# A selective-scan stage in which layer-norm sums are kept as interleaved pairs of token chunks, one normalization is folded into the last sum, and scan states are carried two at a time

## The chip, the cores and the metric

The kernel runs on 1 core of a Trainium2 chip. The metric is the device time of one execution in microseconds (us), as the median of several runs. A core has five engines that run at the same time, each through a list of its own in fixed order: TensorE (PE, matrix products, with its weight loads as PEld), VectorE (DVE), ScalarE (ACT), GpSimd (POOL) and SyncE (SP, which here only starts transfers). An instruction waits on semaphores that other engines raise.

## What is computed

4096 tokens of width 256 go through two layers. The change touches only the last stage: the second layer's selective scan, its output projection, a layer norm, then a feed-forward network with its own input norm, and a last layer norm. Cut to that stage, the reference is:

```
xz = x @ w_in.T + b_in; x_ssm, z = split(xz); z = silu(z)
dt = softplus(x_ssm @ w_dt.T + b_dt); Bm, Cm = x_ssm @ w_B.T + b_B, x_ssm @ w_C.T + b_C
h[t] = exp(A * dt[t]) * h[t-1] + dt[t] * Bm[t] * x_ssm[t]        # for each of 16 states n
y[t] = sum over n of h[t] * Cm[t];  y = (y + D * x_ssm) * z
x = layernorm(y @ w_out.T + b_out + x) * gamma + beta            # "norm3"
x = x + (the same x)   ->  x = layernorm(...)                    # "norm4" (the block's input is added)
h = layernorm(x) * ln_gamma + ln_beta                            # "norm5"
x = layernorm(x + (x + 0.5 * (silu(h @ W1 + b1) @ W2 + b2)))     # "norm6"
```

## The kernel before

The stage works in `NB` = 8 blocks of `TB` = 512 tokens. A block has `NC` = 4 chunks of 128 tokens. Two layouts occur: channels on partitions (two halves k of 128 channels, so a tile of 128 x 2 x 512) for the scan, and tokens on partitions (128 x 4 chunks x 256) for the norms.

For each of the `NS` = 16 states n of block b these steps run:

- GpSimd, `into(b, n)` (L2489): state = u * Bm[n], one instruction of 128x1024. It may not start before the product that last read this state buffer is done and that buffer's last column has been saved. There are 3 buffers, so it waits for product n-3.
- ScalarE, `decay(b, n, k)` (L1870): exp(A * dt) for each half k, into one PSUM bank per half, so it waits for the scan of state n-1 on the same half. `spread_C(b, n)` (L1875) copies the row Cm[n] to the one bank `bank_c`, after product n-1.
- VectorE, `scan(b, n, k)` (L2219) for each half, 128x512; then `product(b, n)` (L2225), 128x1024, into one of two buffers `prod`.
- ScalarE, `carry(b, n)` (L1879): saves the last column of the state for the next block in `h0`.
- TensorE, `add_up(b, n)` (L1654): adds the turned product to `bank_y`; product n+2 waits for it.

Around this each block needs: the projections for the next block (`x_proj`, `d_proj`, `bc_proj`, `z_proj` on TensorE, `evac_*` on ScalarE); softplus, shared by ScalarE (`soft_exp`, `plus_one`, `soft_log`, `minus_one`) and GpSimd (`soft_add`, `soft_fix`, `soft_sum`, and `drive`, which makes u); silu of z and the gate (`silu_z` L1926, `gate` L2231); `d_term` (L1645), `turn_gated` (L1662), `evac_gated` (L1931) and `out_proj`; and the norms. For a norm, VectorE takes `bn_stats` of each chunk and `bn_aggr` of each result, GpSimd makes scale and shift (`norm3`, `norm6` of four tiny steps, `norm45` of ten), ScalarE applies them, and GpSimd applies gamma, beta and the added input (`shifted` L2494, `scaled` L2553, `summed` L2559). Last comes `up_proj`, `silu_up` (L1964), `down_proj` and `second` (L2263).

The order on each engine is written out by hand, in a loop over iterations in which blocks at different ages (`cur`, `post`, `last`, `old`) are interleaved. Exp, Silu and Ln need different tables on ScalarE; each change of table is an instruction ACT_TABLE_LOAD, put in where the order of functions asks for it. After the loop, the last block is finished in halves by the `end_*` functions.

## Time and profile before

| | us |
|---|---|
| median of 3 runs | 1187.65 (1184.77 to 1187.85) |
| the profiled execution | 1185.47 |
| its span | 1183.4 |
| PE busy in the span | 1045.4 (88%) |
| DVE busy | 959.9 (81%) |
| ACT busy | 893.4 (75%) |
| POOL busy | 738.1 (62%) |

The span runs from the first to the last instruction; 2.1 us of the execution lie outside it. Busy shares are averages over stages. The changed stage takes the time from 572.7 us to the end.

### The profile page before, as it was taken

The page shows a single profiled execution, that of the slowest core. Times are in us where ns is not written, and L with a number is a line of the kernel's source. Part 1 is how long each engine was busy: PE and PEld are TensorE (multiplying, and loading weights), DVE is VectorE, ACT ScalarE, POOL GpSimd, SP SyncE. Part 2 cuts the span into 40 slices and gives each one's busy share as a digit, 9 for nine tenths or more (in the row PEclk, how much of TensorE's full clock was granted, in tenths as well). Part 3 has the DMA queues.
Part 4 walks back from the last instruction along what each step waited for, and adds up shares of the span by engine and source line. Part 5 has one row for each costly group of instructions (what it writes and reads, how often), then busy time and mean ns, then how long its engine had stood idle before and what let it go on. Part 6 is the DMA issues. An engine that isn't in the chain of part 4 may idle for free. (4 is left out here: it accounts for less than half of the span.)

```text
span 1183.4 us, 17445 instructions
## 1 busy us (share of the span) xinstructions
PE 1045.4 (88%) x5234; PEld 698.0 (59%) x5234; DVE 959.9 (81%) x1319; ACT 893.4 (75%) x1697; POOL 738.1 (62%) x638
## 2 busy tenths in 40 slices
PE   5999999999968999998476599999999999988987
PEld 4677677676753334444245357667575766756576
DVE  5999999999962576545689989999999999999741
ACT  7878787887644455556777889999898999986743
POOL 1546554654560443534568997979889897988420
PEclk9999999999998999999678899999999999999899
DMA  4543434323405001112866546556565565645201
GB/s 128 153 135 109 122 104 130 112 82 114 126 29 180 1 18 54 37 36 91 211 137 172 123 136 150 143 135 149 151 143 139 151 158 135 148 133 142 67 5 36
DMA packets 93232, 133.83 MB, mean 113 GB/s; under 512 B 8786, under 2 KB 47698, under 8 KB 93140
## 3 DMA queue, kind: packets, MB, share of 16 engines
q1 hardware_dynamic: 93140, 132.73, 41.6%
q8 instruction: 42, 0.69, 0.2%
q14 instruction: 50, 0.41, 0.1%
HBM read 116.45 MB, written 14.16 MB: 110 GB/s over the span
## 5 line engine op out<-in xcount | busy, mean ns | idle before, releaser
L2219 DVE TENSOR_TENSOR_SCAN state<-bank_a,h,state 128x512 f32<-128x512 f32 x256 | 316.4, 1270 | 27.5 <-POOL state L2489 12.4
L2489 POOL TENSOR_TENSOR state<-uc,Bb 128x1024 f32<-128x1024 f32 x64 | 150.7, 2367 | 35.3 <-DVE prod L2225 25.9
L2489 POOL TENSOR_TENSOR state<-s,Bb 128x1024 f32<-128x1024 f32 x64 | 150.7, 2367 | 28.2 <-DVE prod L2225 19.7
L1654 PE MATMUL bank_y<-ident,prod 128*128 128x128 f32 x1024 | 138.5, 282 | 28.5 <-DVE prod L2225 28.4
L1654 PEld LDWEIGHTS bank_y<-ident,prod 128*128 128x128 f32 x1024 | 122.8, 145 | 68.3 <-DVE prod L2225 35.8
L2225 DVE TENSOR_TENSOR prod<-state,bank_c 128x1024 f32<-128x1024 f32 x128 | 154.2, 1204 | 6.4 <-ACT bank_c L1875 4.2
L1699 PE MATMUL bank_m<-w,f_h 128*128 128x256 f32 x448 | 106.1, 387 | 0.0
L39 PE MATMUL bank_m<-nT,w 128*128 128x512 f32 x224 | 103.8, 602 | 0.9 <-ACT nT L1953 0.9
L1870 ACT ACTIVATE bank_a<-s,A 128x512 f32<-128x512 f32 x128 | 86.2, 680 | 12.6 <-DVE state L2219 12.5
L1870 ACT ACTIVATE bank_a<-dtc,A 128x512 f32<-128x512 f32 x128 | 86.4, 681 | 10.4 <-DVE state L2219 10.2
L1699 PEld LDWEIGHTS bank_m<-w,f_h 128*128 128x128 f32 x448 | 83.5, 192 | 15.8 <-issue 5.8
L1875 ACT ACTIVATE bank_c<-Cb 128x512 f32<-128x512 f32 x128 | 75.2, 588 | 15.1 <-DVE prod L2225 15.0
L668 DVE TENSOR_TENSOR_SCAN L<-abc,zeros,b_id 128x512 f32<-128x512 f32 x64 | 78.4, 1267 | 5.8 <-POOL xd L871 3.6
L1309 DVE TENSOR_SCALAR cS<-cS,slope,shift 128x512 f32<-128x512 f32 x24 | 13.1, 545 | 67.5 <-ACT cS L1221 67.5
L39 PEld LDWEIGHTS bank_m<-nT,w 128*128 128x128 f32 x224 | 40.8, 193 | 39.0 <-issue 37.4
L333 PE MATMUL b_op<-W_out,zs 128*128 128x256 f32 x256 | 63.1, 389 | 0.0
L896 POOL TENSOR_TENSOR rms<-ssn,mhalf 128x1 f32<-128x1 f32 x32 | 17.8, 555 | 63.8 <-DVE ssn L697 63.8
L635 DVE SCALAR_TENSOR_TENSOR b_p<-raw,columns,b_p 128x512 f32<-128x512 f32 x72 | 54.1, 752 | 1.3
L871 POOL TENSOR_TENSOR xd<-xs,L 128x512 f32<-128x512 f32 x32 | 33.9, 1059 | 31.6 <-PE b_new L321 15.1
L39 PE MATMUL c<-h,nets 128*128 128x512 f32 x96 | 46.7, 609 | 3.7 <-ACT h L1202 3.6
L39 PE MATMUL b_p<-uh,W_h 128*128 128x512 f32 x132 | 46.8, 436 | 2.8 <-DVE ul L721 2.1
L333 PEld LDWEIGHTS b_op<-W_out,zs 128*128 128x128 f32 x256 | 46.2, 190 | 4.9
(388 smaller groups left out, 2595.9 us busy)
## 6 DMA issues: line engine op xcount, KB each, us to landing
Bb<-CB_rows SPq DMA_DIRECT2D x128, 256.0 KB, 4.1
Cb<-CB_rows SPq DMA_DIRECT2D x128, 256.0 KB, 4.7
abc<-decays SPq DMA_DIRECT2D x32, 512.0 KB, 4.7
Ebc<-ramps SPq DMA_DIRECT2D x64, 128.0 KB, 3.2
uT<-in_uT SPq DMA_DIRECT2D x8, 512.0 KB, 4.3
u<-in_u SPq DMA_DIRECT2D x8, 512.0 KB, 4.3
x_tokens<-x2s SPq DMA_DIRECT2D x8, 512.0 KB, 2.9
x_rows<-x1T SPq DMA_DIRECT2D x8, 512.0 KB, 2.7
```

The costliest lines, as they stand in the source:

```text
L39: i = e.matmul(out, w, x, start=(n == 0), stop=(n == len(pairs) - 1))
L333: i = e.matmul(b_op[:, 0:DM], zs[b % 2][:, m, ts], W_out[:, m, :], start=(m == 0), stop=(m == MD - 1))
L635: e.scalar_tensor_tensor(to, raw[:, m, t:t + TB], cw[:, m, t:t + 1], acc[:, :], ALU.mult, ALU.add).then_inc(v_conv, 1)
L668: e.tensor_tensor_scan(L[:, hs, :].rearrange("p h t -> p (h t)"), abc[g % 2][:, hs, :].rearrange("p h t -> p (h t)"), b_id[:, :], zeros[:, ...
L871: e.tensor_tensor(heads(xd[:, :]), heads(xs[g % 2][:, :]), L[:, :, CH - 1:CH].to_broadcast([P, NH, HD]), ALU.mult).then_inc(p_xd, 1)
L1654: i = e.matmul(p_y[c // 2][:, at:at + P], prod[n % 2][:, k, c * CH:(c + 1) * CH], ident[:, :], start=False, stop=(n == NS - 1), is_transpo ...
L1699: i = e.matmul(to, f_h[:, k, c * CH:(c + 1) * CH], w2[:, k, :], start=False, stop=(c % 2 == 1 and k == KF - 1))
L1870: e.activation(p_a[k][:, :], dtc[b % 2][:, k, :], ACT.Exp, scale=A[:, k, n:n + 1]).then_inc(a_a, 1)
L1875: e.activation(p_c[:, :], Cb[n % 4][:, :], ACT.Copy).then_inc(a_c, 1)
L2219: e.tensor_tensor_scan(s[:, k, :], p_a[k][:, :], s[:, k, :], h0[:, n, k:k + 1], ALU.mult, ALU.add).then_inc(v_s, 1)
L2225: e.tensor_tensor(prod[n % 2][:, :, :], state[(NS * b + n) % 3][:, :, :], both(p_c[:, :]), ALU.mult).then_inc(v_g, 1)
L2489: e.tensor_tensor(state[at % 3][:, :, :], uc[b % 2][:, :, :], both(Bb[n % 4][:, :]), ALU.mult).then_inc(p_b, 1)
```

## The change

It edits the scan stage only and does five things.

1. The tiles `xl` and `x3b` hold two token chunks interleaved word by word (2 pairs x 256 features x 2 chunks). One `bn_stats` over the 512 words of a pair then yields the statistics of both chunks, since that instruction reports even and odd elements apart. Six `bn_stats` of 512 take the place of twelve of 256 per block, and the twelve `bn_aggr` go. Whoever writes or reads one chunk of these tiles does it with a step of two words (8 bytes): `residual`, `second`, norm3, norm5, norm6, `scaled`, `summed`.
2. `norm4` is no longer applied by ScalarE. `second` multiplies `xl` by the per-token scale `rs4d` (twice rs4) while it adds; the constant shift drops out of the last norm. It becomes four instructions of 128x256 with a scale read from a column, instead of two of 128x512 with the constant 2.0. One tiny step (`rs4d`) is added to GpSimd's `norm45`. `xl` gets a second buffer.
3. There are 4 state buffers instead of 3 (`into` waits for product n-4), and `carry` saves two states with one instruction, after the odd one's scan; `into` waits for the pair. A wait on a carry covers both of its states.
4. The last norm writes a tile of its own, `x4`.
5. The order is a new one on all five engines.

The diff, cut:

```diff
-            state, prod = many("state", [P, KD, TB], 3), many("prod", [P, KD, TB])
+            states, prod = t("states", [P, 4, KD, TB]), many("prod", [P, KD, TB])
+            state = [states[:, i, :, :] for i in range(4)]
+            rs4d = many("rs4d", [P, NC])
...
+            xl_twos, x3b_twos = [t(n, [P, 2, DM, 2])[:, :, :, :] for n in ("xl0", "xl1")], t("x3b", [P, 2, DM, 2])[:, :, :, :]
+            xl, x3b = [x.rearrange("p q f c -> p q c f") for x in xl_twos], x3b_twos.rearrange("p q f c -> p q c f")
...
                 def carry(b, n):
-                    e.wait_ge(v_s, 2 * (NS * b + n) + 2)
-                    e.activation(h0[:, n, :], state[(NS * b + n) % 3][:, :, TB - 1], ACT.Copy).then_inc(a_hs, 1)
+                    at = NS * b + n
+                    e.wait_ge(v_s, 2 * at + 4)
+                    e.activation(h0[:, n:n + 2, :], states[:, at % 4:at % 4 + 2, :, TB - 1], ACT.Copy).then_inc(a_hs, 1)
...
-                def norm4(b, p):
-                    e.wait_ge(p_l4, 9 * b + 9)
-                    after(e, v_x3b, 2 * b)
-                    for c in (2 * p, 2 * p + 1):
-                        e.activation(x3[:, c, :], xl[:, c, :], ACT.Identity, bias=nb4[:, c:c + 1], scale=rs4[:, c:c + 1]).then_inc(a_x3, 1)
...
-                def stats4(b, c):
+                def stats4(b, p):
                     e.wait_ge(p_add, b + 1)
-                    e.bn_stats(st4[:, c, :], xl[:, c, :]).then_inc(v_l4, 1)
-
-                def mean4(b, c):
-                    e.wait_ge(v_l4, 8 * b + c + 1)
-                    e.sem_inc(step, 1)
-                    e.bn_aggr(mv4[:, c, :], st4[:, c, :]).then_inc(v_l4, 1)
+                    after(e, p_l4, 9 * b)
+                    e.bn_stats(st4[:, p, :], both_of(xl_twos[b % 2], p)).then_inc(v_l4, 1)
 
                 def second(b, p):
                     e.wait_ge(pe_dn, 2 * b + p + 1)
-                    e.wait_ge(a_x3, 4 * b + 4)
-                    after(e, st_o, DMAS * b)
-                    e.scalar_tensor_tensor(x3b[:, 2 * p:2 * p + 2, :].rearrange("p c f -> p (c f)"), x3[:, 2 * p:2 * p + 2, :].rearrange("p c f -> p (c f)"),
-                                           2.0, pair[p][:, :], ALU.mult, ALU.add).then_inc(v_x3b, 1)
+                    after(e, a_n6, 4 * b)
+                    for c in (0, 1):
+                        at = 2 * p + c
+                        i = e.scalar_tensor_tensor(one(x3b, at), one(xl[b % 2], at), rs4d[b % 2][:, at:at + 1], pair[p][:, c * DM:(c + 1) * DM], ALU.mult, ALU.add)
+                    i.then_inc(v_x3b, 1)
...
                 def into(b, n):
...
-                    after(e, v_g, at - 2)
-                    after(e, a_hs, at - 2)
+                    after(e, v_g, at - 3)
+                    after(e, a_hs, (at - 4) // 2 + 1)
...
                     e.tensor_tensor(rs5[:, :], rs4[:, :], sq4[:, :], ALU.mult)
+                    e.tensor_scalar(rs4d[b % 2][:, :], rs4[:, :], 2.0, None, ALU.mult)
...
                 def scaled(b):
                     e.wait_ge(a_n3, 4 * b + 4)
                     e.sem_inc(step, 1)
-                    e.tensor_tensor(xl, xl, rowwise(gam), ALU.mult).then_inc(p_gam, 1)
+                    e.tensor_tensor(xl[b % 2], xl[b % 2], every(gam), ALU.mult).then_inc(p_gam, 1)
```

Below, the order at three places of a block, once before and once in the change. Names are those of tiles without buffer numbers; `x2`, `x3` read as `x`, `st3` as `st`, `s12` as `s`.

GpSimd, first part of a block, before: five `into`, then `shifted` (x<-x), norm6, an `into`, norm3.

```order
L2489 TENSOR_TENSOR state<-s,Bb 128x1024 x5
L2494 TENSOR_TENSOR x<-x,everywhere 128x1024
L2513 TENSOR_SCALAR ve<-mv 128x4
L2516 TENSOR_TENSOR rs<-ve,mhalf 128x4
L2519 TENSOR_TENSOR nb<-mv,rs 128x4
L2522 TENSOR_SCALAR nb<-nb 128x4
L2489 TENSOR_TENSOR state<-s,Bb 128x1024
L2499 TENSOR_SCALAR ve<-mv 128x4
```

In the change:

```order
L2432 TENSOR_TENSOR states<-s,Bb 128x1024 x6
L2437 TENSOR_TENSOR x<-x,everywhere 128x1024
L2442 TENSOR_SCALAR ve<-st 128x4
L2445 TENSOR_TENSOR rs<-ve,mhalf 128x4
L2448 TENSOR_TENSOR nb<-st,rs 128x4
L2451 TENSOR_SCALAR nb<-nb 128x4
L2432 TENSOR_TENSOR states<-s,Bb 128x1024 x2
```

A sixth `into` moved ahead of `shifted`, and norm6 (L2513 to L2522) moved away from here.

GpSimd, from the end of norm45 to the first `into` of the next block, before: `into` 11, `soft_add`, `into` 12 and 13, `soft_fix`, 14, `soft_sum`, 15, `drive`, and on.

```order
L2548 TENSOR_TENSOR nb<-nb,sq 128x4
L2489 TENSOR_TENSOR state<-s,Bb 128x1024
L2564 TENSOR_TENSOR s<-s 128x1024
L2489 TENSOR_TENSOR state<-s,Bb 128x1024 x2
L2570 TENSOR_TENSOR s<-s,uc 128x1024
L2489 TENSOR_TENSOR state<-s,Bb 128x1024
L2576 TENSOR_TENSOR dtc<-dtc,s 128x1024
L2489 TENSOR_TENSOR state<-s,Bb 128x1024
L2582 TENSOR_TENSOR uc<-dtc,xc 128x1024
L2489 TENSOR_TENSOR state<-uc,Bb 128x1024 x5
```

In the change, after the two `into` that now follow norm45:

```order
L2508 TENSOR_TENSOR s<-s 128x1024
L2432 TENSOR_TENSOR states<-s,Bb 128x1024
L2456 TENSOR_SCALAR ve<-st 128x4
L2459 TENSOR_TENSOR rs<-ve,mhalf 128x4
L2462 TENSOR_TENSOR nb<-st,rs 128x4
L2465 TENSOR_SCALAR nb<-nb 128x4
L2432 TENSOR_TENSOR states<-s,Bb 128x1024 x2
L2514 TENSOR_TENSOR s<-s,uc 128x1024
L2432 TENSOR_TENSOR states<-s,Bb 128x1024
L2520 TENSOR_TENSOR dtc<-dtc,s 128x1024
L2526 TENSOR_TENSOR uc<-dtc,xc 128x1024
L2432 TENSOR_TENSOR states<-uc,Bb 128x1024 x6
```

Between norm45 and the next block's first `into` there is one `into` more (number 10), and norm6 (L2456 to L2465) now stands here.

ScalarE, the silu functions of a block, before (`silu_up` three times, `silu_z`, `spread_C`, `silu_up`, then the table of Exp again):

```order
L1964 ACT_TABLE_LOAD
L1964 ACTIVATE f_h<-f_h 128x1024 x3
L1926 ACTIVATE zgs<-zgs 128x1024
L1875 ACTIVATE bank_c<-Cb 128x512
L1964 ACTIVATE f_h<-f_h 128x1024
L1870 ACT_TABLE_LOAD
```

In the change:

```order
L1948 ACT_TABLE_LOAD
L1948 ACTIVATE zgs<-zgs 128x1024
L1980 ACTIVATE f_h<-f_h 128x1024
L1896 ACTIVATE bank_c<-Cb 128x512
L1891 ACT_TABLE_LOAD
```

and 13 rows further on:

```order
L1980 ACT_TABLE_LOAD
L1980 ACTIVATE f_h<-f_h 128x1024 x3
L1896 ACTIVATE bank_c<-Cb 128x512
L1891 ACT_TABLE_LOAD
L1891 ACTIVATE bank_a<-dtc,A 128x512
```

One stretch became two, with two table loads more per block; the 13 rows between them are the next scans' work (six `decay`, two evacuations each of gT and xc, `spread_C`, two `carry`).

## Rows read from the trace of the kernel before

**Rows 1.** Busy time by engine, one steady block; the first line names the columns.

```profile
core 0: us, PE busy (x) PEld busy (x) DVE busy (x) ACT busy (x) POOL busy (x), PEclk, DMA share, GB/s
915.50:984.40 68.90, 65.27 (x317) 45.67 (x316) 65.54 (x79) 64.34 (x115) 60.72 (x41) 1.00 0.61 149
```

**Rows 2.** Instructions on bank_y, the gates: ns min/median/max, first and last start.

```profile
L2231 DVE TENSOR_TENSOR zgs<-bank_y,zgs x16: 662/679/691, 640.1 to 1121.0; 128x512 f32<-128x512 f32 x16
```

**Rows 3.** Chain that ended last: start us, us, what.

```profile
874.47 2.39 POOL xl L2559
```

**Rows 4.** Timeline of POOL: start us, us, instruction, count [idle before <-releaser].

```profile
852.55 2.37 POOL L2489 TENSOR_TENSOR state<-uc,Bb 128x1024 f32<-128x1024 f32 x1 [2.89 <-DVE prod L2225]
854.88 2.37 POOL L2494 TENSOR_TENSOR x<-x,everywhere 128x1024 f32<-128x1024 f32 x1
...
860.48 2.37 POOL L2489 TENSOR_TENSOR state<-uc,Bb 128x1024 f32<-128x1024 f32 x1 [0.89 <-ACT h L1879]
862.94 0.23 POOL L2499 TENSOR_SCALAR ve<-mv 128x4 f32<-128x4 f32 x1
...
865.18 4.71 POOL L2489 TENSOR_TENSOR state<-uc,Bb 128x1024 f32<-128x1024 f32 x2
...
881.60 0.23 POOL L2527 TENSOR_SCALAR ve<-mv 128x4 f32<-128x4 f32 x1
...
886.68 2.36 POOL L2489 TENSOR_TENSOR state<-uc,Bb 128x1024 f32<-128x1024 f32 x1
...
907.83 7.03 POOL L2489 TENSOR_TENSOR state<-s,Bb 128x1024 f32<-128x1024 f32 x3 [0.20 <-POOL s L2582]
```

**Rows 5.** Timeline of DVE, the first row one block earlier than the others.

```profile
841.19 3.63 DVE L2219 TENSOR_TENSOR_SCAN state<-bank_a,h,state 128x512 f32<-128x512 f32 x3
...
860.22 2.56 DVE L2219 TENSOR_TENSOR_SCAN state<-bank_a,h,state 128x512 f32<-128x512 f32 x2 [0.93 <-ACT h L1879]
...
878.91 1.38 DVE L2252 BATCH_NORM_STATS2 st<-xl 128x6 f32<-128x256 f32 x4
880.21 0.41 DVE L2257 BATCH_NORM_AGGREGATE mv<-st 128x2 f32<-128x6 f32 x4
```

**Rows 6.** Groups by line: count | busy us, mean ns | idle before, releasers.

```profile
L2225 DVE TENSOR_TENSOR prod<-state,bank_c 128x1024 f32<-128x1024 f32 x128 | 154.2, 1204 | 6.4 <-ACT bank_c L1875 4.2 <-PE bank_y L1654 0.6 <-DVE state L2219 0.2
...
L2263 DVE SCALAR_TENSOR_TENSOR x3b<-x,bank_m 128x512 f32<-128x512 f32 x14 | 9.5, 683 | 1.6 <-PE bank_m L1699 1.6
...
L1879 ACT ACTIVATE h<-state 128x2 f32<-128x2 f32 x128 | 24.7, 193 | 1.5 <-DVE state L2219 1.5
```

**Rows 7.** Groups by line, the first layer's residual, whose scale is a column.

```profile
L704 DVE SCALAR_TENSOR_TENSOR r<-b_op,rms,u 128x256 f32<-128x256 f32 x32 | 15.2, 475 | 4.6 <-POOL rms L896 4.6
```

**Rows 8.** Timeline of ACT: evacuations of gT, silu functions and table loads, norm5.

```profile
846.81 1.08 ACT L1931 ACTIVATE gT<-bank_m 128x512 f32<-128x512 f32 x2 [0.22 <-PE bank_m L1662]
...
849.08 0.58 ACT L1875 ACTIVATE bank_c<-Cb 128x512 f32<-128x512 f32 x1
...
851.42 1.28 ACT L1964 ACT_TABLE_LOAD   x1
...
859.39 0.69 ACT L1870 ACTIVATE bank_a<-dtc,A 128x512 f32<-128x512 f32 x1
...
886.76 2.07 ACT L1942 ACTIVATE xn<-xl,nb,rs 128x256 f32<-128x256 f32 x4 [1.25 <-POOL nb L2548]
```

**Rows 9.** Timeline of PE: `turn_gated` and `d_term`.

```profile
846.06 1.09 PE L1662 MATMUL bank_m<-ident,zgs 128*128 128x128 f32 x8
...
852.56 1.95 PE L1645 MATMUL bank_y<-diagD,xc 128*128 128x128 f32 x16
```

**Rows 10.** Groups by line, an earlier stage in which POOL and DVE both read two SBUF tiles.

```profile
L1326 DVE TENSOR_TENSOR ob<-oa,tw 128x512 f32<-128x512 f32 x8 | 13.1, 1638 | 0.3
...
L1416 POOL TENSOR_TENSOR oa<-oa,tw 128x512 f32<-128x512 f32 x8 | 12.4, 1552 | 34.2 <-DVE tw L1314 34.0
```

**Rows 11.** Timeline of PE: three pieces of `down_proj` in a row.

```profile
876.97 5.45 PE L1699 MATMUL bank_m<-w,f_h 128*128 128x256 f32 x24
```

636 lines of the change are left out of this document (288 added, 348 removed).

## The prediction, made before the result was known

> **What bounds the kernel now.** I read the busy time by block first. In a steady block of 68.9 us PE is busy 65.3, DVE 65.5, ACT 64.3 and POOL 60.7 us, at a PE clock of 1.00 [rows 1]. No engine is full and three are above 93%, so the question is which loop closes last. The gates run once per block, the first at 640.1 and the last at 1121.0: seven intervals, 68.7 us each on average [rows 2]. Then the chain of waits: it goes through ACT's silu stretch, DVE, and from `summed` on through POOL without a break to the next block's first scan [rows 3]. POOL's timeline shows the loop. Before `shifted` POOL waits 2.89 us for a product, and then 0.89 us for a carry [rows 4]; from 881.60, where norm45 starts, it never waits for another engine: norm45 takes 5.1 us, then ten instructions of 2.33 us (a state after another starts so far apart: 7.03 for three) end at 907.83 + 2.35 = 910.2, and the next block's first scan starts there. With the scan's start at 841.19 [rows 5] as zero, the loop reads: 40.4 us until norm45 + 5.1 + 23.5 = 69.0 us, the block. So POOL, the least busy engine, sets the period by the second half of its list, and DVE, ACT and PE idle 3 to 5 us each. What counts is when norm45 can start, and what stands behind it.
>
> **The change, part by part** (per block; no transfer is added, and the loads' waits for `into` come earlier).
>
> *Statistics.* Four bn_stats take 1.38 us, (1.38 - 0.41) / 3 = 0.325 apart; four bn_aggr 0.41, about 0.09 apart [rows 5]. Twelve of each: 3.9 + 1.1 = 5.0 us. The 512-wide form is not in the trace. Below it lies the 256-wide one (0.325), above two of them (0.65); I take 0.60, the pitch of the 512-wide 0.683 us addition less an overlap of 0.08 [rows 6]. Six: 3.6 us. Gain 1.4, bounds 1.1 to 3.0.
>
> *`second`.* Two of 0.683 become four with a column as scale; that form took 475 ns [rows 7], 0.40 apart. 4 x 0.40 - 2 x 0.60 = +0.4. DVE gains 1.0 us: 64.5.
>
> *ACT.* norm4 goes: four of the kind of norm5, 2.07 for four [rows 8], -2.0. Eight carries of 0.193 us [rows 6], which cost their 0.10 pitch, go: -0.8. Two table loads come: 1.28 each [rows 8], and since nothing overlaps with one, 1.39; +2.8. ACT stays at 64.3: the loads eat what the norm gave.
>
> *POOL.* One tiny step in norm45, +0.17. PE: nothing but its order.
>
> *Steps of 8 bytes.* No wide instruction of the trace steps over words. Below: nothing (a gain has no cause, the words are as many). Above: the dearest rows of such a kind, where both engines fight for SBUF: a 512-wide DVE instruction 1.64 us instead of 0.68, a 512-wide POOL one 1.55, so 3.10 for 1024 words against 2.37 [rows 10, 4]. I take nothing, since the nearest row, the same instruction without a step, knows no such rival here; the upper end is a rival below.
>
> The Trainium skill speaks against that choice in one place: *Vector Engine (DVE) Microarchitecture Reference*, section "Measured stream behaviour on trn2", states that a port streams at full rate only in runs of two adjacent words, and that a hop at every word costs about 0.65 cycle; its page *SBUF — State Buffer*, section "Door 1: The DMA port swizzle", says that fp32 may be strided up to four words for free. By the first `residual` and `second` would cost DVE some 1.6 us more per block (an estimate from that page) and eat its gain, with ACT and POOL perhaps alike, which is the last rival below; by the second they would cost nothing. No row here decides.
>
> *The loop, anew.* Zero is again the block's first scan. (a) DVE's list to product 5: 16 scans at (3.63 - 1.27) / 2 = 1.18 = 18.9; six products at 1.12 (1.204 less 0.08) = 6.7; gates, residuals and norm3's statistics, two each at 0.60 = 3.6; half of `second` 0.8. Together 30.0. Into it come waits. The gates end at 3.65; then PE runs `d_term` 1.8 (moved ahead of `turn_gated`), and turns 1.1 [rows 9], so at 6.0 ACT evacuates gT, with decays between, then `spread_C` and the first pair's carry: 3.05 us (the like stretch took 849.66 - 846.81 = 2.85, [rows 8]), until 9.05. Two decays and an evacuation more: 10.9. Then ACT's second silu stretch: load, three silus, `spread_C`, load = 6.2 us (the one before took 8.0, 851.42 to 859.39) until 17.1, so the next scan starts at 17.8. DVE's own list gets there at 16.8: 1.0 us of wait, in place of the 0.93 there [rows 5]. Two waits of 0.2 for decays before that. Product 4 waits for `add_up` 2, which PE has behind four pieces of `down_proj`, 7.3 us (three take 5.45, [rows 11]), and a `d_proj`: 0.6. Decay 7 stands behind `soft_exp`: 0.2. The last two are my reading of two lists side by side, good to half a microsecond each. Sum 2.2, so product 5 ends at 32.2. (b) POOL: `into` 4 waits for the pair's carry at 9.05, `into` 5 follows, `shifted` at 13.8 (before: 854.88 - 841.19 = 13.7), norm3 to 18.4 (2.24, [rows 4]), `into` 6 and 7, `scaled`, `summed`, `into` 8 = 5 x 2.33, with 1.25 of waits for product 3 and ACT's norm3: 31.5. So `into` 9 waits for product 5: 32.2. What stood in the way before, norm6 and an `into` between `shifted` and norm3, 865.18 - 857.3 less norm3 = 5.6 us, is gone. (c) From there: `into` 9 2.33, norm45 5.25, then 11 wide instructions 25.6 and norm6 2.25: 67.7. Norm6, free before because it stood where POOL waits, is now paid on the path, and so is `into` 10.
> I add 0.3 for handovers that I didn't count: **68.0 us a block, 1.0 less** than the 69.0 that the same reckoning gives before. Four buffers alone gain nothing there: the path runs over carry and norm45, not over a state buffer.
>
> *Sum.* Seven intervals: -7.0. First block: silu_z's loads come before its second state instead of its third, the softplus part has more products to run behind it: -0.5. End: after the last matmul 2 bn_aggr (0.25 with their handovers) and half a bn_stats overlap go, the two-part `second` costs 0.2 more [rows 5 to 7]: -0.3. Together -7.8. The profiled execution was 1185.47, its span 1183.4; the median stands 2.2 above it. On the median: 1187.65 - 7.8 = 1179.9, rounded **1180**.
>
> **Rivals.**
> *POOL alone (faster).* If DVE's four waits shrink, `into` 9 starts at 31.5 at once and the handovers cost nothing: 67.0 us, 2.0 less, 1187.65 - 14 - 0.8 = 1173. For it: each wait is small, and PE's share (65.3) allows it. If it packs better still, PE's 65.3 is the floor: 1162.
> *No change.* The loop gains nothing if the waits in (a) are 3.2 instead of 2.2, with three engines above 93%: two silu stretches leave DVE without decays twice. Then 68.7 to 69.0: 1186 to 1188.
> *The pair's carry (slower).* `into` 4 waits for a carry which in ACT's list stands behind both gT evacuations, these behind `turn_gated`, that behind `d_term` and the gates. A carry at 9.05 is just right; from 10.1 on the block is as long as before, since all of (b) follows it 1:1 once POOL passes product 5. Were it at 11.5, the block would be 69.4, and a late `into` 4 also starts the scans later: +0.5 x 7 and more, 1192. POOL's wait of 2.89 us at this place [rows 4] shows how much hangs there.
> *The steps cost (slower).* `scaled` and `summed` lie on POOL's path; at 3.10 instead of 2.37 the block grows by 1.5, ACT's four norm3 and DVE's second `residual` add 0.5: 2.0 x 7 = 14, less 7.8: 1194. It decides from 0.5 us per pass, a fifth of its 2.37.
> The Trainium skill's DVE page, section "Measured stream behaviour on trn2", points this way.
>
> **How the numbers follow.** A measurement of this kernel tells about 0.3% (3.6 us) from no change. Forecast (1174 to 1184) 0.40; POOL alone and better 0.18; no change 0.18; pair's carry 0.12; steps 0.12. Faster 0.58, same 0.18, slower 0.24. The range leaves out half of the two outer ends: 1168 to 1195.
>
> **What would show it.** A gate interval near 68.0; norm45 starting some 35 us after a block's first scan instead of 40.4, and the first scan still waiting for its `into` (POOL) at the block's end; norm6 among POOL's unbroken work; 6 table loads per block; DVE near 64.5 busy, ACT unchanged. `scaled` at 2.37 and `residual` at 0.68 prove the steps free. I'm wrong in my main step if the first scan doesn't wait for POOL, or if norm45 starts later than 36 or earlier than 33.

## The result, and the profile after

The changed kernel takes 1193.01 us, the kernel before 1187.22 in the same measurement: a ratio of 1.0048, 95% interval 1.0035 to 1.0060. It is 0.5% slower; I had forecast 0.6% faster (1180). The profiled execution of the changed kernel took 1192.86, its span 1190.9, 7.5 more than the 1183.4 of before. (The profiled execution of one experiment, old_order_s6, ran at a lower clock throughout, so the trace read in its place is that of the same kernel made again, old_order_s6_b.)

Two windows of the changed kernel, each from gates to gates. The columns are those of [rows 1]:

```profile
core 0: us, PE busy (x) PEld busy (x) DVE busy (x) ACT busy (x) POOL busy (x), PEclk, DMA share, GB/s
853.30:922.40 69.10, 65.85 (x314) 45.32 (x314) 64.14 (x64) 64.27 (x105) 61.12 (x42) 1.00 0.53 146
922.40:993.20 70.80, 67.34 (x314) 46.99 (x314) 64.18 (x63) 64.67 (x105) 61.08 (x42) 0.98 0.61 142
```

The same view in windows of 5 us, one row of it:

```profile
925.00:930.00 5.00, 5.00 (x21) 3.76 (x20) 3.27 (x3) 3.13 (x6) 3.95 (x2) 0.69 0.64 126
```

DVE fell from 65.5 us [rows 1] to 64.15, a little more than I said, and ACT stayed. But a clean block takes 69.08, not 68.0, and one block takes 70.8: in it PE's granted clock was 0.69 for five microseconds, between its two levels.

The difference of 7.5 us, by place, from the first scan and the gates in the two timelines, one profiled execution of each kernel:

| Stretch | before | after | difference | forecast |
|---|---|---|---|---|
| start of the stage's first scan | 575.27 | 576.13 | +0.9 | 0 |
| from there to the first gates | 64.8 | 71.3 | +6.5 | -0.5 |
| seven intervals of gates | 480.3 | 481.8 | +1.5 | -7.0 |
| last gates to the end of the span | 63.0 | 61.6 | -1.4 | -0.3 |

The seven intervals hold a first one that is 0.9 longer (67.7 against 66.8), one dip of the clock (+2.1 against before), a last interval that is 2.0 shorter, and otherwise blocks of 69.08 instead of 68.8 to 69.1. The start of the stage moved between 573.0 and 579.4 in the experiments, whatever they changed: that 0.9 is no part of the change. One execution is a coarse measure of the second row too: without a stall this stretch took 62.7 to 65.6 us in the experiments, and 63.2 and 65.6 in two executions of one kernel (old_order and its repeat). The medians below say the same with less noise.

**The first block.** PE, ACT, DVE and POOL of the changed kernel at the start of the stage. Columns: start us, us, instruction, count, [idle before <- what ended it]:

```profile
584.10 3.78 PE L39 MATMUL bank_m<-xT,w_xz 128*128 128x512 f32 x4 [15.30 <-DMA xT<-x_rows]
587.68 3.15 PE L1667 MATMUL bank_y<-diagD,xc 128*128 128x128 f32 x16
```

```profile
580.31 1.30 ACT L1891 ACTIVATE bank_a<-dtc,A 128x512 f32<-128x512 f32 x2
590.86 0.69 ACT L1908 ACTIVATE xc<-bank_m,columns 128x512 f32<-128x512 f32 x1 [9.25 <-PE bank_y L1667]
```

```profile
581.11 2.46 DVE L2219 TENSOR_TENSOR_SCAN states<-bank_a,h,states 128x512 f32<-128x512 f32 x2 [1.26 <-ACT bank_a L1891]
592.23 2.46 DVE L2219 TENSOR_TENSOR_SCAN states<-bank_a,h,states 128x512 f32<-128x512 f32 x2 [8.67 <-ACT bank_a L1891]
```

```profile
593.65 4.69 POOL L2432 TENSOR_TENSOR states<-uc,Bb 128x1024 f32<-128x1024 f32 x2 [10.86 <-ACT h L1901]
```

Four engines stand still. In the new list of PE `x_proj(1, 0)` stands ahead of `d_term(0)`; it needs the second block's `xT`, which lands at 584.1. ACT's evacuation of it (L1908) waits for `d_term(0)` and stands ahead of decay 2, DVE's scan 2 waits for that decay, and POOL for a carry.

**A clean block.** DVE from its first scan to product 5, and POOL from `into` 2 to norm45, in the changed kernel:

```profile
850.91 2.46 DVE L2219 TENSOR_TENSOR_SCAN states<-bank_a,h,states 128x512 f32<-128x512 f32 x2 [1.08 <-POOL states L2432]
...
868.84 2.46 DVE L2219 TENSOR_TENSOR_SCAN states<-bank_a,h,states 128x512 f32<-128x512 f32 x2 [0.83 <-ACT h L1901]
...
877.85 1.22 DVE L2225 TENSOR_TENSOR prod<-states,bank_c 128x1024 f32<-128x1024 f32 x1 [0.62 <-PE bank_y L1676]
...
882.81 1.22 DVE L2225 TENSOR_TENSOR prod<-states,bank_c 128x1024 f32<-128x1024 f32 x1 [0.19 <-PE bank_y L1676]
```

```profile
855.11 4.70 POOL L2432 TENSOR_TENSOR states<-uc,Bb 128x1024 f32<-128x1024 f32 x2 [1.97 <-ACT h L1901]
860.45 4.69 POOL L2432 TENSOR_TENSOR states<-uc,Bb 128x1024 f32<-128x1024 f32 x2 [0.65 <-ACT h L1901]
...
884.20 2.38 POOL L2432 TENSOR_TENSOR states<-uc,Bb 128x1024 f32<-128x1024 f32 x1 [1.13 <-issue]
886.66 0.19 POOL L2470 TENSOR_SCALAR ve<-st 128x4 f32<-128x4 f32 x1
```

The shape is the forecast one. With the first scan at 850.91 as zero, `into` 4 starts at 9.5 (forecast 9.05), `into` 9 waits for product 5 (the row with 1.13; the trace names no releaser, but the product ended at 884.03, 0.17 earlier), norm45 starts at 35.75 (34.55; 40.4 before), and from there POOL runs on to the next first scan, which waits for it (1.08). But product 5 ends at 33.1, not 32.2, and behind norm45 (4.8; forecast 5.25) POOL needs 28.4, not 27.9.

PE in the same block of the changed kernel:

```profile
854.60 2.05 PE L1667 MATMUL bank_y<-diagD,xc 128*128 128x128 f32 x16 [1.90 <-DVE zgs L2231]
856.49 1.04 PE L1684 MATMUL bank_m<-ident,zgs 128*128 128x128 f32 x8
...
867.95 7.17 PE L1721 MATMUL bank_m<-w,f_h 128*128 128x256 f32 x32
874.96 1.88 PE L39 MATMUL bank_m<-xc,w_dt 128*128 128x512 f32 x4
876.68 1.04 PE L1676 MATMUL bank_y<-ident,prod 128*128 128x128 f32 x8
```

From `d_term` on none of its rows has a wait. The last row is `add_up` 2, for which product 4 waits: 23.1 us of PE work stand between the gates and product 4. The next `add_up` ends 5.0 us of PE work later, and product 5 waits for it in turn (0.19).

### The profile page after: what moved, and what is told of

Read it like the earlier page. It is cut to its first block and busy times, and to the rows that moved or that the text cites. A ratio compares the mean times of both kernels' runs of the same rounds, so it can differ in the third digit from the quotient of the medians.

```text
span 1190.9 us, 17184 instructions
## 1 busy us (share of the span) xinstructions
PE 1053.6 (88%) x5234; PEld 705.4 (59%) x5234; DVE 948.9 (80%) x1193; ACT 888.6 (75%) x1613; POOL 739.8 (62%) x645
## 5 line engine op out<-in xcount | busy, mean ns | idle before, releaser
L2219 DVE TENSOR_TENSOR_SCAN states<-bank_a,h,states 128x512 f32<-128x512 f32 x256 | 315.2, 1268 | 35.1 <-ACT bank_a L1891 24.2
L2432 POOL TENSOR_TENSOR states<-uc,Bb 128x1024 f32<-128x1024 f32 x64 | 150.5, 2367 | 36.1 <-ACT h L1901 19.3
L2225 DVE TENSOR_TENSOR prod<-states,bank_c 128x1024 f32<-128x1024 f32 x128 | 154.2, 1205 | 19.0 <-PE bank_y L1676 11.3
L2432 POOL TENSOR_TENSOR states<-s,Bb 128x1024 f32<-128x1024 f32 x64 | 150.5, 2366 | 22.6 <-ACT h L1901 13.4
L1676 PEld LDWEIGHTS bank_y<-ident,prod 128*128 128x128 f32 x1024 | 122.2, 146 | 58.3 <-DVE prod L2225 27.9
L1721 PE MATMUL bank_m<-w,f_h 128*128 128x256 f32 x448 | 102.4, 382 | 0.0
L39 PEld LDWEIGHTS bank_m<-nT,w 128*128 128x128 f32 x224 | 39.7, 190 | 39.7 <-issue 34.9
```

What stands on the lines that cost most here:

```text
L39: i = e.matmul(out, w, x, start=(n == 0), stop=(n == len(pairs) - 1))
L1676: i = e.matmul(p_y[c // 2][:, at:at + P], prod[n % 2][:, k, c * CH:(c + 1) * CH], ident[:, :], start=False, stop=(n == NS - 1), is_transpo ...
L1721: i = e.matmul(to, f_h[:, k, c * CH:(c + 1) * CH], w2[:, k, :], start=False, stop=(c % 2 == 1 and k == KF - 1))
L2219: e.tensor_tensor_scan(s[:, k, :], p_a[k][:, :], s[:, k, :], h0[:, n, k:k + 1], ALU.mult, ALU.add).then_inc(v_s, 1)
L2225: e.tensor_tensor(prod[n % 2][:, :, :], state[(NS * b + n) % 4][:, :, :], both(p_c[:, :]), ALU.mult).then_inc(v_g, 1)
L2432: e.tensor_tensor(state[at % 4][:, :, :], uc[b % 2][:, :, :], both(Bb[n % 4][:, :]), ALU.mult).then_inc(p_b, 1)
```

## Experiments

Each kernel was timed beside the kernel before (here with its own ratio), and "block us" is the usual interval of gates among the middle five of its profiled execution, those with a dip of the clock left out.

| Kernel | median us | ratio, 95% | block us |
|---|---|---|---|
| changed kernel | 1193.0 | 1.0048 (1.0035 to 1.0060) | 69.08 |
| fix_first | 1185.1 | 0.9978 (0.9962 to 0.9995) | 69.06 |
| before_stall | 1193.9 | 1.0053 (1.0033 to 1.0073) | 68.8, 69.1 |
| fix_x_twice | 1186.5 | 1.0000 (0.9984 to 1.0016) | 69.08 |
| fix_norm6 | 1183.8 | 0.9960 (0.9946 to 0.9975) | 68.8 |
| fix_silu | 1196.6 | 1.0071 (1.0045 to 1.0098) | 69.8; three with a dip, 71.1 to 71.4 |
| fix_norm6_silu | 1190.3 | 1.0023 (1.0006 to 1.0039) | 69.65 |
| fix_silu22 | 1188.6 | 1.0018 (1.0002 to 1.0034) | 69.08, 69.4, 69.85; two with a dip |
| fix_norm6_silu22 | 1186.2 | 1.0004 (0.9990 to 1.0019) | 69.7 |
| fix_single | 1188.4 | 1.0008 (0.9992 to 1.0023) | 69.06 |
| before_four | 1180.9 | 0.9949 (0.9933 to 0.9964) | 68.04 |
| before_four_pairs | 1180.1 | 0.9941 (0.9926 to 0.9956) | 67.98 |
| before_four_into5 | 1182.7 | 0.9953 (0.9936 to 0.9970) | 68.01 |
| old_order | 1179.8 | 0.9949 (0.9929 to 0.9969) | 67.84 |
| old_order_b, the same again | 1182.0 | 0.9956 (0.9939 to 0.9973) | 67.83 |
| old_order_into5 | 1182.5 | 0.9966 (0.9954 to 0.9978) | 67.84 |
| old_order_s6 | 1183.5 | 0.9963 (0.9948 to 0.9978) | not read |
| old_order_s6_b, the same again | 1182.4 | 0.9962 (0.9948 to 0.9977) | 67.74 |
| old_order_three | 1186.0 | 0.9983 (0.9969 to 0.9997) | 68.33 |

**1. The first block.** One kernel takes the early projection back in the first block alone, the other puts it, in the first block alone, into the kernel before.

```diff
# fix_first: PE of the changed kernel (x_proj(1, 1) and d_proj(1, ...) likewise, and ACT's evacuations to match)
-                    if 0 < cur < NB:
+                    if 1 < cur < NB:
                         x_proj(cur, 0)
                     if live(post):
                         d_term(post)
...
                     if live(post):
                         add_up(post, 0)
+                    if cur == 1:
+                        x_proj(cur, 0)
```

```diff
# before_stall: PE, then ACT, of the kernel before
+                    if cur == 1:
+                        x_proj(cur, 0)
                     if live(post):
                         d_term(post)
...
+                    if nxt == 1:
+                        evac_x(nxt, 0)
                     if live(cur):
                         carry(cur, 0)
                         decay(cur, 2, 0)
```

> The changed kernel, but in the first block alone PE does x_proj(1,0) after add_up(0,0) and x_proj(1,1) after add_up(0,1) (and d_proj(1,0), (1,1) after add_up 2 and 3), and ACT evacuates them behind carry(0,2), decay(0,5,0), decay(0,6,0) and carry(0,4), roughly as the kernel before did. Theory A (a load at the head of the line: x_proj(1,0) waits for the xT load until 584.1 and holds d_term(0), add_up(0,0), ACT's decay 2, DVE and POOL): the first gate comes at 640 to 641.5 instead of 647.4, the median falls by 6 to 7.5 us to 1186 +- 1, the same as the kernel before. Rival B (the first block is long because of silu_z's early table loads and the carries in pairs, which stay): the first gate stays at 645 to 648 and the time at 1191 to 1193.

> The kernel before, with one move in the first block alone: x_proj(1,0) ahead of d_term(0), and its evacuation ahead of ACT's carry(0,0) and decay(0,2,0). Theory A: the first gate moves from 640.1 to 646 to 648 and the time rises by 6 to 8 us, to about 1194. Rival B (the load's wait is hidden, and something else in the new order costs): 1187 to 1189, first gate at 640 to 642.

fix_first is 0.7% below the changed kernel's ratio, and from its first scan (575.78) to its first gates (641.0) it takes 65.3 us instead of 71.3; 64.8 was before's. before_stall rises from 1187.2 to 1193.9; from its first scan (579.40) to the first gates (652.8) it takes 73.4, in an execution (1198.2) that was 4 us above its median. Its trace has the same rows: PE, then ACT.

```profile
587.88 3.44 PE L39 MATMUL bank_m<-xT,w_xz 128*128 128x512 f32 x4 [15.17 <-DMA xT<-x_rows]
```

```profile
593.14 0.69 ACT L1888 ACTIVATE xc<-bank_m,columns 128x512 f32<-128x512 f32 x1 [10.56 <-PE bank_y L1645]
```

One instruction placed ahead of its data, once in the run, costs 6.6 us in the one kernel and about 8 in the other, by the medians: more than the whole difference between the two. silu_z's early table loads (rival B) cost nothing that stands clear of the spread of this stretch.

**2. The dips of the clock.** fix_x_twice computes `x_proj(b, 0)` twice from block 2 on, where PE waits 1.90 us for the gates:

```diff
+                    if m == 0 and b > 1:
+                        passes(e, single[:, :], [(w_xz[...], xT[:, k, :]) for k in range(KD)])
                     passes(e, single[:, :], [(w_xz[...], xT[:, k, :]) for k in range(KD)]).then_inc(pe_x, 1)
```

> fix_first, with x_proj(b, 0) of the blocks 2 to 7 computed twice in a row (the second overwrites the first; four 128x512 matmuls, 1.88 us at 2.4 GHz, behind add_up 15), where PE waits 1.90 us for the gates. Theory C (a clean block costs 69.07 whatever PE does there, and the two dips to 1.2 GHz behind that wait, 1.5 and 1.75 us in two blocks, come because PE stands still): no interval above 69.3 among the third to the sixth, which saves about 3.3 us in a profiled run; the median 1 to 3 us below fix_first's 1185.1. Rival Q (PE's work is the bound): each block grows by up to 1.9, and the time rises by 5 to 12 us. Rival D (the dips come whatever PE does): intervals of 70.6 stay, time within 1 us of fix_first.

fix_first's profiled execution had two blocks of 70.6 and 70.8; in fix_x_twice the same blocks are 69.09 and 69.39 (a little above the 69.3 of theory C), with a clock of 1.00, and the wait is 0.19 instead of 1.90:

```profile
918.29 2.05 PE L1669 MATMUL bank_y<-diagD,xc 128*128 128x128 f32 x16 [0.19 <-DVE zgs L2249]
```

So 1.9 us more of PE work there is free (rival Q falls). The other traces speak for theory C as well. Five kernels have a PE wait of 1.9 to 2.2 us at the gates from their third block on (the changed kernel, fix_first, fix_silu, fix_silu22, fix_single); 9 of their 20 blocks of this kind show a dip, each right behind the gates. The other profiled kernels wait about 1.0 us or less there (fix_x_twice, the three with norm6 moved, all that have the order of before), and none of their middle blocks shows one. But the median of fix_x_twice is 0.2% above fix_first's, not below. What the dips cost on average stays open. What one dip does is plain, and it matters below. DVE in the changed kernel's block with the clock at 0.69:

```profile
948.43 1.22 DVE L2225 TENSOR_TENSOR prod<-states,bank_c 128x1024 f32<-128x1024 f32 x1 [0.62 <-PE bank_y L1676]
```

Product 4 comes 28.43 us after this block's first scan (920.00) instead of 26.94, still with 0.62 us of wait for PE: what PE loses to the clock between the gates and `add_up` 2 (1.5 us), the block loses (1.8 in all).

**3. What closes the loop in the new order.** All with the first block mended. fix_norm6 moves POOL's norm6 out of the tail behind norm45 to where POOL waits 1.97 us; fix_silu merges ACT's two stretches of silus (two table loads fewer per block); fix_norm6_silu does both; silu22 moves one silu from the second stretch to the first; fix_single saves each state by itself, the first of a pair earlier.

```diff
# fix_norm6, POOL (ACT's second norm6 goes behind spread_C 3)
                         into(cur, 1)
+                    if 0 <= old < NB - 2:
+                        norm6(old)
...
                         into(cur, 12)
-                    if 0 <= last < NB - 2:
-                        norm6(last)
# fix_norm6, ACT
                         decay(cur, 1, 1)
+                    if 0 <= old < NB - 2:
+                        norm6(old, 0)
...
                         evac_x(nxt, 0)
```

```diff
# fix_silu, ACT
-                        silu_z(cur)
-                        silu_up(last, 0)
...
+                        silu_up(last, 0)
                         silu_up(last, 1)
                         silu_up(last, 2)
                         silu_up(last, 3)
+                        silu_z(cur)
```

> fix_first, and POOL's norm6 of block b moved from behind into 12 of block b+2 to behind into 1 of block b+3, where POOL waits 1.97 us for a carry; ACT's norm6 ahead of evac_x (1.27 us of wait there) and behind spread_C 3. Theory P (POOL still closes the loop: the block's first scan waits 1.08 us for it): the 2.25 us of norm6 leave POOL's saturated half, the interval between gates falls from 68.9 by about 1.1 to 67.8, where DVE or PE takes over, so about 7 us below fix_first: 1179. Rival Q (PE, 65.9 us busy with a 1.9 us wait for the gates in each block and clock dips after it, already sets the period): the interval stays at 68.6 to 69.0 and the time at 1185 to 1187.

> fix_first, with silu_z and silu_up 0 moved from the block's start into the second stretch of silus: one stretch of load, five silus, load instead of two, so two table loads fewer per block (2.6 us of ACT). If the long stretch starves DVE (it lasts 1.28 + 3.9 + 1.06 + 1.28 = 7.5 us and more instead of 6.2, but nothing stands ahead of the first scan): scan 4 comes about 1.3 to 2 us later and the interval grows by 0.5 to 1.2 us: time 1190 to 1194. If ACT's total is what binds: interval 67.5 to 68, time 1178 to 1180. If neither, within 2 us of fix_first.

> fix_norm6 with the silus in one stretch, as fix_silu had them (interval 71.1). Theory T (in the new order ACT's stretch, product 5, into 9, norm45 and the 13 steps behind it are one loop, so its terms add): norm6 gone from the tail takes 2.0 to 2.25 off 71.1, interval 68.9 to 69.2, time 1184 to 1187. Rival U (the stretch closes a loop of its own through scan, gates and gT, in which norm6 has no part): 70.5 to 71.2, time 1194 to 1197.

> fix_first, with silu_up 1 in ACT's first stretch of silus instead of the second: stretches of 3 and 2 silus instead of 2 and 3, table loads as many. In the changed kernel scan 4 waits 0.83 us behind the second stretch, while ACT waits 1.27 us for PE behind the first. If the loop runs through ACT's second stretch to product 5, into 9 and norm45: interval 69.07 - 0.5 to 0.8 = 68.3 to 68.6, 3 to 5 us below fix_first: 1180 to 1182. If the carry into 2 (then 0.95 later) or another wait takes over: within 1.5 us of fix_first.

> fix_norm6 with the same move of silu_up 1. There POOL no longer closes the loop (its carry wait at into 13 is 1.21 us), and DVE waits 0.34, 0.94, 0.82 and 0.45 us for ACT in the first 22 us of a block. If it is ACT's second stretch that holds DVE: scan 4's 0.82 goes, interval 68.75 - 0.8 = 68.0, time 1178 to 1179. If ACT's whole list up to soft_exp is what holds DVE (no ACT wait stands in it but 0.32): the wait only moves between the stretches, 68.6 to 68.9, time 1183 to 1185.

> fix_first with a carry for each state instead of each pair (8 more per block on ACT, 0.8 us), carry 14 ahead of silu_z and carry 0 ahead of the evacuations of gT, so that into 2 (1.97 us of wait) and into 4 (0.65) can run earlier. If the pair's late release is what binds (theory K): interval 68.0 to 68.5, time 1179 to 1182. If product 5 and what comes behind it bind (into 9 waits 1.13 us for it in a clean block): POOL's waits move to shifted and into 9, interval 69.0 to 69.4, time within 2 us of fix_first.

*norm6 off the tail.* 69.06 becomes 68.8, not 67.8, and the median is 1.3 us below fix_first's, not 7. But this kernel did two things at once. On POOL 2.25 us left the tail, and the first scan no longer waits for POOL; DVE's list has taken over, and from product 5 to the next first scan it takes 34.9 us instead of 36.0. On ACT the first half of norm6 (1.12 us) moved ahead of the evacuation of `x_proj`, and now PE waits for that evacuation in a stretch that had no wait. PE, then DVE, in fix_norm6 (first scan at 842.50):

```profile
849.86 1.98 PE L39 MATMUL bank_m<-xT,w_xz 128*128 128x512 f32 x4 [0.75 <-ACT xc L1916]
```

```profile
870.28 1.22 DVE L2241 TENSOR_TENSOR prod<-states,bank_c 128x1024 f32<-128x1024 f32 x1 [0.58 <-PE bank_y L1676]
```

Product 4 starts 27.8 us after the first scan instead of 26.9. So 1.1 us were won behind product 5 and 0.8 lost ahead of product 4; the 0.3 are the difference, and no run shows norm6 moved on POOL alone. fix_norm6_silu22, which missed both of its expectations, puts one silu more ahead of the same evacuation. PE in it (first scan at 840.96):

```profile
849.26 1.98 PE L39 MATMUL bank_m<-xT,w_xz 128*128 128x512 f32 x4 [1.69 <-ACT xc L1916]
```

Product 4 starts at 28.7, and the block grows from 68.8 to 69.7, by what product 4 came later.

*One stretch of silus.* At full clock the block is 69.8, 0.75 longer than fix_first's. The 71.1 on which the expectation of fix_norm6_silu was built is a block with a dip of the clock; three of this kernel's five middle blocks had one. Two windows of fix_silu, one with a dip and one without, columns as in [rows 1]:

```profile
849.35:920.53 71.18, 67.29 (x314) 46.91 (x314) 63.81 (x63) 62.00 (x102) 61.09 (x42) 0.98 0.54 142
991.59:1061.39 69.80, 64.11 (x310) 44.72 (x310) 63.81 (x64) 61.79 (x102) 61.07 (x42) 1.00 0.54 137
```

With norm6 moved as well a block takes 69.65, without a dip: 0.15 less than 69.8, not 2.0 to 2.25. So neither theory T nor rival U is borne out, and the two table loads saved brought nothing. In both kernels with one stretch DVE waits ahead of product 4 for the later silus (1.80 us ahead of product 2, 0.83 ahead of scan 4), and product 4 no longer waits for PE.

*The other two.* Moving a silu took away scan 4's wait and put 1.55 us ahead of scan 2; single carries took away POOL's wait ahead of `into` 2 and put 2.31 ahead of `into` 4. fix_single's blocks stayed at 69.0 to 69.1 bar one dip, and the shortest of fix_silu22 is 69.08. Their ratios are 0.3 and 0.4% above fix_first's all the same; fix_silu22 had blocks of 69.4 and 69.85 besides, and for fix_single the trace doesn't show why. DVE in fix_silu22 (a block with a dip; in one without, product 4 waits 0.62 too), then in fix_single:

```profile
848.51 2.46 DVE L2235 TENSOR_TENSOR_SCAN states<-bank_a,h,states 128x512 f32<-128x512 f32 x2 [1.55 <-ACT bank_a L1899]
...
868.04 1.22 DVE L2241 TENSOR_TENSOR prod<-states,bank_c 128x1024 f32<-128x1024 f32 x1 [0.62 <-PE bank_y L1676]
```

```profile
870.87 1.22 DVE L2251 TENSOR_TENSOR prod<-states,bank_c 128x1024 f32<-128x1024 f32 x1 [0.62 <-PE bank_y L1676]
```

In every kernel that kept two stretches of silus, product 4 waits for PE: 0.62 in the changed kernel, in its block with the slow clock, with a silu moved and with single carries, 0.58 in fix_norm6. So the loop reads: gates, PE's 23.1 us to `add_up` 2, product 4, product 5, `into` 9, norm45, POOL's 28.4, first scan, gates. What ACT, DVE or the carries gain ahead of product 4 doesn't shorten it as long as PE doesn't wait for them. Made longer, PE's part shows in the block each time: by a dip (product 4 1.5 us later), by ACT's norm6 (0.8) and by norm6 and a silu (1.8). That a shorter list of PE there would give the time back was not run; this half is argued, not shown.

**4. Buffers and carries alone.** The kernel before with four state buffers; the same with the carries in pairs; the same with `into` 5 behind `into` 4:

```diff
-            state, prod = many("state", [P, KD, TB], 3), many("prod", [P, KD, TB])
+            state, prod = many("state", [P, KD, TB], 4), many("prod", [P, KD, TB])
...
-                    after(e, v_g, at - 2)
-                    after(e, a_hs, at - 2)
+                    after(e, v_g, at - 3)
+                    after(e, a_hs, at - 3)
```

> The kernel before with four state buffers instead of three, nothing else. My prediction: nothing gained there, since its loop runs over the carry and norm45; interval 68.6 to 68.9, time 1186.5 to 1188. Rival: POOL's waits for a product before into are on the path (2.89 us before shifted), and a fourth buffer takes one of them away: interval lower by 0.5 to 2 us, time 1175 to 1184.

> The kernel before with four state buffers (an interval of 68.03 us) and the carries in pairs, each pair at the place of its odd carry in ACT's list; nothing else. Theory K (the pair gives back what the fourth buffer brought, since slot and carry are released two states at a time, and the interval of the changed kernel, 69.09, is 1.05 above that of before_four for it): interval 68.8 to 69.3, time 1186 to 1190. Rival L (POOL has 3.24 us of idle time ahead of shifted, which takes a later release; the 8 carries fewer give ACT 0.8 us): interval 67.9 to 68.2, time 1179 to 1182, and the 1.05 lies in the order and the two more table loads of the changed kernel.

> before_four with into 5 moved from behind norm6 to behind into 4, where POOL waits 3.24 us for a residual. POOL's unbroken run, from norm6 to the next block's scans, gets 2.35 us shorter. If POOL closes the loop of before_four (one wait of 0.52 us of DVE for a state is left in it): the interval falls until DVE's own list binds, 65.5 us of work and 1.9 of waits for ACT and PE: 67.4 to 67.6, about 3.5 us less in all, 1176 to 1178. If DVE binds there already: 68.0, within 1 us of before_four.

My statement that four buffers alone gain nothing is wrong: they give 0.8 us a block and 0.5%. POOL in before_four:

```profile
849.73 2.39 POOL L2494 TENSOR_TENSOR x<-x,everywhere 128x1024 f32<-128x1024 f32 x1 [3.24 <-DVE xl L2238]
```

The waits for a product and a carry of [rows 4] (2.89 and 0.89) are gone; what is waited for is the residual, and then the statistics of norm6 (1.31). norm45 starts 0.8 us earlier after the first scan, at 39.6. The carries in pairs, my slower rival, cost nothing: the release comes later (a new wait of 1.36 for a carry), and the 3.24 shrink to 1.81. `into` 5 moved into that gap brings nothing either: 0.47 us of wait for the statistics appear ahead of norm45.

**5. The new instructions in the old order.** old_order is the changed kernel (its buffers, statistics, `second`, carries in pairs) with every engine's list in the order of before up to the end of the loop: an instruction that is gone is left out, and a statistic of a pair stands where those of its chunks stood. Behind the loop its lists are those of the changed kernel. The other three move one to three entries of it:

```diff
# s6, DVE
                         scan(post, 10, 0)
-                    if 0 <= old < NB - 2:
-                        stats6(old, 0)
...
                         stats3(post, 1)
+                    if 0 <= old < NB - 2:
+                        stats6(old, 0)
# into5, POOL; "three" has both, and norm4's statistics ahead of scan(post, 8, 1)
                         into(cur, 4)
+                        into(cur, 5)
                     if 0 <= post < NB - 1:
                         shifted(post)
```

> The changed kernel's buffers and instructions (interleaved pairs, one statistics instruction for each, norm4 in the last sum, carries in pairs, four states), but every engine's list in the order of the kernel before, first block included. Theory O (the new order is what costs, the new instructions bring the 1.0 us of DVE that I predicted): norm45 can start earlier by what DVE saves ahead of it, 0.6 to 1.0, so an interval of 67.1 to 67.5 against 68.0 for before_four_pairs, time 1174 to 1177. Rival Y (the new instructions cost on the path what they save, by steps of 8 bytes or by waits): 68.0 or more, time 1180 or more. Rival P (POOL's unbroken run from norm6 on, which does not depend on DVE's savings, holds it at 68.0): 67.9 to 68.1.

> old_order with into 5 behind into 4, ahead of shifted, where POOL waits for a residual. If POOL's run from norm6 on held old_order, 0.5 to 1.0 us per block less than that, 1170 to 1174. If DVE's list up to the statistics of norm4 holds it, no change (within 1.5 us of old_order), as it was for before_four_into5.

> old_order_s6 again. Theory S (the saved work had been cover): DVE's wait for decay 4 is 1.1 to 1.2 us, the interval 67.2 to 67.4, 3 to 4 us less than old_order on the same chip. Rival (the next wait takes it up: the median of the disturbed run, 1184.5, points this way): interval 67.7 to 68.2, the time within 2 us of old_order.

> old_order_s6 with into 5 ahead of shifted, and the statistics of norm4 one scan (1.2 us) earlier in DVE's list, ahead of scan(8,1). If two loops hold the block, both are eased now: norm45 can start up to 1.2 us earlier, and DVE's list with its waits is 64.4 + 2.7 = 67.1: interval 67.0 to 67.4, a gate sum about 3 to 4 us below old_order's, time 1177 to 1179. If ACT's norm3 ahead of scaled (1.8 us of wait there in old_order_into5) or another wait holds it: 67.6 to 67.9, within 1.5 us of old_order.

old_order takes 67.84, 0.14 less than before_four_pairs, though DVE has 0.9 us less to do (64.4 busy against 65.25). Where it went, in its DVE:

```profile
855.78 2.47 DVE L2212 TENSOR_TENSOR_SCAN states<-bank_a,h,states 128x512 f32<-128x512 f32 x2 [1.81 <-ACT bank_a L1887]
```

The wait for the decay behind ACT's stretch of silus has grown from 0.93 (in before_four and in before_four_pairs) to 1.81. From the gates (840.30) to this scan it is 15.48 us, and in before_four (840.85 to 856.33) the same 15.48: all that the statistics and `second` save ahead of scan 4 is waited away there. Moving another statistic there (s6) cut the wait to 1.38 and the block to 67.74: 0.1, not 0.6, because DVE then waits 0.71 for POOL's last states; its median is that of old_order's repeat. `into` 5 ahead of `shifted` changes nothing (67.84). Both together, with norm4's statistics earlier, gave 68.33 (old_order_three), worse: now ACT waits 1.61 us for PE's turned gates, where it waited 0.95 in old_order.

```profile
844.59 1.09 ACT L1949 ACTIVATE gT<-bank_m 128x512 f32<-128x512 f32 x2 [1.61 <-PE bank_m L1679]
```

old_order's block is shorter than that of before_four_pairs, yet the kernel isn't faster: from the last gates to the end it takes 66.9 us (66.9 to 67.2 in all five executions of this family), where before_four_pairs takes 63.5 and the changed kernel 61.6. The end part and the lists were not written for each other. ACT's list behind the loop is the changed kernel's, with two silus ahead of the last evacuation of the gates; before has them behind it. In the changed kernel the table load and the silus begin before the last gates, in old_order ACT first has norm6 to do at that point, and PE waits for the evacuation, 3.66 us where before_four_pairs has 0.77:

```profile
1116.87 0.79 PE L1622 MATMUL bank_c<-bias,ones 64*128 64x512 f32 x1 [3.66 <-ACT gT L1988]
```

DVE's first instruction behind it starts 10.2 us after the last gates instead of 5.3 (changed kernel 4.7). The 3.4 us that its end is longer than that of before_four_pairs come from there, as far as these rows show; a kernel with before's order there wasn't run. Its block is what speaks about the new instructions, not its median.

## Why the prediction was wrong

*The first block, -0.5; measured +6.5.* This is the step that failed and that by itself decides the sign: I read the new order of PE and ACT in a steady block, where `xT` is there, and carried it over to the block in which it isn't. The term of the sum, "First block: ... -0.5", looked at table loads and products; whether an instruction that moved up finds its data there was checked for the steady state alone. The row to ask was the load's: when does the second block's `xT` land, against the start of the stage (584.1 against 573)? fix_first and before_stall show it: about 8 us less and 6.6 more.

*DVE's list to product 5, end at 32.2; measured 33.1.* I did name the wait of product 4 for `add_up` 2 and put it at 0.6, which is what it measured (0.62). The whole list measured 30.6 us of work and 2.6 of waits, where I had 30.0 and 2.2: a wait of 0.38 for `down_proj` ahead of `second` was not foreseen, and each wait takes away the 0.08 by which an instruction of DVE otherwise starts before its predecessor ends. But the error that matters is another. I added the waits of DVE one after another, as if each were a price; the last wait on the list absorbs all those ahead of it. The end of product 5 is the later of two chains, and the one through PE was never added up: gates at 3.7, `d_term` moved ahead of `turn_gated`, 23.1 us of PE without a gap, product 4 at 26.9, product 5 to 33.1.

*`into` 9 to the next first scan.* `into` 9 with its handover took 2.6 instead of 2.33, norm45 4.8 instead of 5.25, the rest 28.4 instead of 27.9: two handovers of 0.2 around `drive` and 0.1 ahead of norm6 were not counted one by one. (In (b) the terms add up to 31.3, not 31.5; nothing hangs on it, since product 5 comes later.) The claim that norm6 on the tail is paid holds for at most 1.1 of its 2.25 us, since DVE's list comes next; fix_norm6 got 0.3 of it, because ACT's part of the move cost 0.8.

*"Four buffers alone gain nothing."* Wrong by 0.8 us a block, which is nearly all that the change has to offer. I followed POOL's unbroken run back to norm45, found `shifted` and norm3 ahead of it, and stopped at the carry's wait of 0.89. That wait and the 2.89 for a product [rows 4] are both waits for a free state buffer. With a fourth buffer both are gone, and of their 3.8 us 0.8 reach norm45; the residual and the statistics take the rest.

*DVE's 1.0 us per block.* About right in size (0.9 in old_order, 1.35 in the changed kernel), worth 0.14. Statistics were the cover of a silu stretch.

*ACT unchanged, the end -0.3, the steps of 8 bytes free.* ACT 64.3 both times; the end gave -1.4; `residual` took 680 ns with its step (682 before), the statistics of 512 words 668 to 681. POOL's `scaled` and `summed` took 0.04 us more each, not 0.73. The two rivals that I feared, pair's carry and steps, didn't come: `into` 4 starts at 9.5, and that they were priced at 1192 and 1194, close to the 1193 measured, is chance.

Put together from the kernels: per block -0.8 from the buffers, -0.14 from the new instructions and +1.24 from the order (67.84 to 69.08), together some +0.2; over seven intervals +1.5, of which a dip is the most; +6.5 in the first block, -1.4 at the end. Had the first block been as before, the change would have been 0.2% faster (fix_first, 0.9978), still well short of the forecast 0.6%. Without the new order it would have been 0.5% faster, and that comes from the fourth buffer.

Best of all measured is before_four_pairs (0.9941, 0.9926 to 0.9956), which beats both kernels; before_four, in which only the number of state buffers and the two waits that go with it differ, is the same within its interval.

## What to carry to other kernels

An order that is right for the steady state has to be read once more for the first pass: each instruction that moved up must have its data there too, and one wait at the head of a queue stops every engine behind it. When waits on one engine are summed, ask which of them would still stand if the earlier ones were gone: the last wait for another engine means that the other engine's chain has to be added up from where both last met. Work taken from an engine inside a stretch where it waits for another one is worth nothing; before a saving is counted, see what it was the cover of. A block with a dip of the clock may not be set against one without. A move that needs a second engine to follow is two experiments in one: look for what the second one stopped. And try the smallest part of a change alone.

## What the runs showed of the hardware

Steps of two fp32 words cost DVE nothing that can be seen. Groups by line of the changed kernel, whole stage (count | busy us, mean ns | idle before):

```profile
L2237 DVE TENSOR_TENSOR xl<-bank_m,x 128x512 f32<-128x512 f32 x14 | 9.5, 680 | 0.0
L2260 DVE BATCH_NORM_STATS2 st<-x3b 128x6 f32<-128x512 f32 x14 | 9.4, 672 | 0.0
L2254 DVE SCALAR_TENSOR_TENSOR x3b<-xl,rs4d,bank_m 128x256 f32<-128x256 f32 x28 | 12.1, 474 | 3.8 <-PE bank_m L1721 3.8
```

`residual` writes with a step and takes 680 ns; in the kernel before, without one, it took 682:

```profile
L2238 DVE TENSOR_TENSOR xl<-bank_m,x 128x512 f32<-128x512 f32 x14 | 9.5, 682 | 1.2 <-PE bank_m L1673 0.8
```

In the changed kernel `second` reads and writes with steps and takes 474, where the like form without took 475 [rows 7]. The other two engines pay a little: POOL's `scaled` and `summed` take 2.41 us each, 2.37 and 2.38 in the kernel before, and ACT's norm3 and norm6 616 ns against 590 and 587. The Trainium skill's page *Vector Engine (DVE) Microarchitecture Reference*, section "Measured stream behaviour on trn2", would have had these hops cost DVE time; the rows here differ, and the measurement decides. Its page *SBUF — State Buffer*, section "Door 1: The DMA port swizzle", which calls strides of up to four words free, agrees.

One instruction of statistics over 512 words takes 668 to 681 ns and stands 0.6 us apart from the next; two of 256 and their two aggregations took 2 x 0.325 + 2 x 0.09 = 0.83 [rows 5]. The pair form is worth 0.23 us each where it is worth anything.

PE's granted clock dips behind a wait of 1.9 to 2.2 us at the gates in some blocks and not in others: in one of the four such blocks of the changed kernel, two of fix_first, three of fix_silu, two of fix_silu22, one of fix_single. No middle block with a wait of about 1.0 us or less there has one, in the fourteen other profiled executions; fix_norm6_silu22, whose PE waits 1.69 us some 6 us behind the gates, has none either. How long a wait it takes was not measured. A dip costs a block 1.3 to 1.8 us, because PE's list behind the gates is on the path.
